# Flamingo block on one core: DVE's selection rounds, the rank matmuls, the roots on GpSimd and SyncE's first loads stand in another order

## The chip, the cores and the metric

The kernel runs on one core of a Trainium2 chip. Its five engines run their own instruction streams: TensorE (PE), VectorE (DVE), ScalarE (ACT), GpSimd (POOL) and SyncE (SP). The metric is device time in microseconds (us) for one execution of the whole program; lower is better.

## The reference

Four gated parts follow each other on `x` of 4 batches x 256 rows x 256 columns: a learned 256 x 256 adjacency per batch, a mixture of 64 experts, a causal attention with 16 heads, and a mixture of 8 experts with a shared one. The change lies in the first two:

```
# adjacency of batch b, h = context, adj_raw = layernorm(x)
threshold = top_k(sim, 76)[..., -1:]
A = sigmoid(sim) * (sim >= threshold)
x = x + tanh(g_xattn[0]) * ((1 - gamma) * layernorm(x) + gamma * (A + A.T) / 2)
# experts, on layernorm(x) as 1024 rows
probs = softmax(xn @ gate_w.T)               # 64 experts
topk_w, topk_idx = top_k(probs, 8)
out = sum over the 8 experts e of  w_e * (silu(xn @ g_e.T) * (xn @ u_e.T)) @ w2_e.T
x = x + tanh(g_ffn[0]) * out
```

## The kernel before

The 1024 rows are `TT` = 8 tiles of 128, two per batch (`BT`). The kernel is written engine by engine, each block in its own order, and the engines meet at named semaphores.

**Routing, per batch b.** PE makes the scores, ACT copies them (`sim_copied`). DVE finds the 76th largest of each row in `ROUNDS` = 10 rounds (`top_rounds`, L1103): a round is a `max` of eight values and a `match_replace` that takes them out, each for two tiles; the last round is a `max` alone. `mask(b)` (L1136) writes `AM`. On PE, `mix(b)` (L526) sums in PSUM the base rows (`ident` times `BASES`), `AM` and `AM` transposed. ACT copies the sum to `X1` (L898, `x1_kept`). `mix_stats(b)` takes mean and variance (`var_ready`), `norm_scale(b)` on POOL takes the root (L432), and `mix_norm(b)` writes the normalised rows `XNA` (L1159). PE's `logits(b)` follows, then DVE's `choose(b)` (L1168), which marks the eight chosen experts of each row in `MB` (bfloat16 zeros and ones, `mask_ready`). PE's `ranks(b)` (L554) counts how many rows ahead of each row chose the same expert: a product of ones with the mask of every earlier tile, and of a strict triangle with its own. `place(b)` (L1180) turns the counts into slot numbers `IDX` (`idx_ready`).

DVE works on the rounds of batch b + 1 in the waits of batch b; the loop at L1199 deals them out by hand. The order of the experts needs the totals `psN` and `psC`, which PE sums at the end over all eight masks (L575 to L579, `counted`).

**Rows to slots.** POOL sends each tile's rows to the slots of their experts in DRAM (`slots_in`), one indirect DMA for each of the eight choices: 16 for a batch, 64 in all (L441 to L449). `norm_scale` of the next batch stands in this stream. A batch's 16 need its `IDX` and `XNA`.

**Experts.** The experts are ordered by load; a place is a position in this order. SP reads the number of the expert at a place (`value_load` of `ORD`, after `order_ready`), loads its weights into `WR` (128 x 768 numbers, L348) and its slots into `XE` (L352). Both are rings of `RING` = 8. The slots wait for all 64 scatters (`scattered`); from the ninth place on, SP waits until the place that held the ring entry is done. For each place PE turns the slots (`flip`, L593), makes gate and up (`gate_up`, L606) and, one place later, down (L616).

Afterwards POOL gathers the results, and attention and the second mixture follow; the change doesn't touch them.

## Time and profile before

| what | value |
|---|---|
| median of 3 runs | 563.95 us (562.79 to 567.25) |
| profiled execution, its own time | 561.23 us |
| its span, first to last instruction | 559.3 us |
| busy: PE, DVE, ACT, POOL | 412.9, 344.4, 184.5, 148.6 us |
| mean granted clock of TensorE | 0.92 |
| first scatter starts, last one starts | 43.22 us, 137.56 us |
| first slots landed, PE starts on them | 142.85 us |

The profile records one execution. Starts are given in us from the span's start; a row of the timeline names engine, line of the kernel, output and inputs, and in brackets how long the engine stood idle before it and what ended that. The profiled execution is 2.7 us shorter than the median of the runs; 1.9 us of its time lie outside its span.

### The profile page before, as it was taken

What the parts mean: (1) busy time and instruction counts of PE and PEld (TensorE: products, weight loads), DVE (VectorE), ACT (ScalarE), POOL (GpSimd) and SP (SyncE); (2) the same over time, 40 slices, a digit from 0 to 9 for tenths busy, and PEclk for the clock granted to TensorE, in tenths of its full rate; (3) what the DMA queues carried; (4) which work ended last, traced back from release to release, by engine and by line L of the source; (5) the groups of instructions that cost most, each with busy time, mean ns of one, the idle gap of its engine ahead of it and who ended that gap; (6) DMA issues with size and microseconds to landing.
All of it is one profiled execution on the core that took longest, in us unless ns stands there. A gap on an engine that the chain in (4) does not pass through costs nothing.

```text
span 559.3 us, 9235 instructions
## 1 busy us (share of the span) xinstructions
PE 412.9 (74%) x2738; PEld 347.8 (62%) x2738; DVE 344.4 (62%) x1053; ACT 184.5 (33%) x377; POOL 148.6 (27%) x156
## 2 busy tenths in 40 slices
PE   5345642500799999999823676799789988998796
PEld 3234441400798888988622554797678867996695
DVE  4988876279334444443346893488667885680664
ACT  3122220100233333343236143524453354427321
POOL 4017775757000000000477723330424000000000
PEclk9999999755699999999965879799999999999999
DMA  7999222237599999999832201110212000000000
GB/s 238 424 416 403 91 94 76 94 112 282 146 293 303 324 317 313 331 355 385 279 98 75 86 22 56 39 39 2 59 39 75 2 0 0 20 1 2 2 19 20
DMA packets 36789, 82.96 MB, mean 148 GB/s; under 512 B 6032, under 2 KB 16144, under 8 KB 34960
## 3 DMA queue, kind: packets, MB, share of 16 engines
q1 hardware_dynamic: 23616, 56.48, 29.2%
q0 software_dynamic: 6144, 16.79, 9.4%
q10 hardware_dynamic: 6992, 9.24, 4.6%
q8 instruction: 17, 0.28, 0.2%
q14 instruction: 20, 0.16, 0.1%
HBM read 50.44 MB, written 31.92 MB: 147 GB/s over the span
## 4 chain that ended last, share of the span: by engine, by line
PE 50%; DVE 13%; issue 12%; POOL 7%; ACT 7%; SPq 4%; DMA 3%; another core or an unknown queue 2%; ACTq 1%; DVEq 0%; POOLq 0%
PE PS L606 9%; POOL slots_in L447 7%; PE PS L616 6%; PE PS L695 5%; PE PS L772 3%; PE PS L708 3%; PE PS L709 3%; PE PS L710 3%; PE PS L593 2%; PE PS L669 2%; DMA XE<-slots_in 2%; PE PS L790 2%; PE PS L800 2%; PE PS L757 2%
## 5 line engine op out<-in xcount | busy, mean ns | idle before, releaser
L454 POOL DMA_INDIRECT GB<-slots_out,IDXG x64 | 70.2, 1096 | 221.1 <-DMA slots_out<-OE 133.3
L606 PE MATMUL PS<-XTE,WR 128*128 128x128 f32 (+2 forms) x512 | 80.5, 301 | 0.0
L447 POOL DMA_INDIRECT slots_in<-XNA,IDX x64 | 64.9, 1014 | 38.3 <-issue 30.8
L606 PEld LDWEIGHTS PS<-XTE,WR 128*128 128x128 f32 x512 | 71.2, 195 | 0.3
L1302 DVE TENSOR_TENSOR HE<-SGE,PS 128x128 f32<-128x128 f32 (+2 forms) x64 | 19.9, 312 | 71.7 <-ACT SGE L927 66.3
L616 PE MATMUL PS<-WR,HE 128*80 128x256 f32 (+2 forms) x198 | 53.3, 380 | 0.5 <-issue 0.5
L918 ACT COPY XTE<-PS 128x256 f32<-128x256 f32 (+2 forms) x64 | 26.3, 410 | 73.1 <-PE PS L593 72.0
L708 PE MATMUL PS<-XH,WGH 128*128 128x256 f32 x160 | 50.3, 314 | 0.0
L593 PE MATMUL PS<-CF,XE 80*128 80x80 f32 (+2 forms) x198 | 28.6, 258 | 26.2 <-DMA XE<-slots_in 26.0
L695 PE MATMUL PS<-WD,XW 128*128 128x256 f32 x160 | 42.6, 389 | 5.8 <-DVE TH L1391 5.8
L593 PEld LDWEIGHTS PS<-CF,XE 80*128 80x128 f32 (+2 forms) x198 | 22.9, 145 | 36.5 <-DMA XE<-slots_in 29.7
L709 PE MATMUL PS<-XL,WGH 128*128 128x256 f32 x160 | 45.5, 284 | 0.0
L710 PE MATMUL PS<-XH,WGL 128*128 128x256 f32 x160 | 45.4, 284 | 0.0
L1295 DVE COPY OE<-PS 128x256 f32<-128x256 f32 (+2 forms) x64 | 36.2, 566 | 8.2 <-PE PS L616 5.5
L979 ACT ACTIVATE AM<-PS 128x256 f32<-128x256 f32 x40 | 15.3, 383 | 68.9 <-PE PS L710 68.8
L1391 DVE SCALAR_TENSOR_TENSOR TH<-PS,CM,TH 128x256 f32<-128x256 f32 x72 | 31.5, 479 | 4.4 <-PE PS L695 3.9
L695 PEld LDWEIGHTS PS<-WD,XW 128*128 128x128 f32 x160 | 27.9, 193 | 9.2 <-DVE XW L1398 4.3
L927 ACT ACTIVATE SGE<-PS 128x128 f32<-128x128 f32 (+2 forms) x64 | 18.9, 296 | 43.9 <-PE PS L606 43.9
L616 PEld LDWEIGHTS PS<-WR,HE 128*80 128x80 f32 (+2 forms) x198 | 30.0, 165 | 5.2 <-issue 0.9
L1473 DVE TENSOR_REDUCE NM<-PS 128x2 f32<-128x256 f32 x64 | 31.6, 549 | 2.4 <-PE PS L775 2.2
L1347 DVE SCALAR_TENSOR_TENSOR BASE<-GB,W,BASE 128x256 f32<-128x256 f32 x56 | 26.7, 485 | 10.1 <-DMA GB<-slots_out,IDXG 5.5
L708 PEld LDWEIGHTS PS<-XH,WGH 128*128 128x128 f32 x160 | 30.9, 193 | 1.1 <-issue 0.6
(226 smaller groups left out, 814.9 us busy)
## 6 DMA issues: line engine op xcount, KB each, us to landing
WR<-in_wexp SPq DMA_DIRECT2D x64, 384.0 KB
slots_in<-GB SPq DMA_DIRECT2D x12, 1024.0 KB, 18.5
XE<-slots_in SPq DMA_DIRECT2D x24, 160.0 KB, 4.4
slots_out<-OE ACTq DMA_DIRECT2D x24, 160.0 KB
XE<-slots_in SPq DMA_DIRECT2D x29, 128.0 KB, 4.3
slots_out<-OE ACTq DMA_DIRECT2D x24, 128.0 KB
WGU<-in_wgu SPq DMA_DIRECT2D x1, 2560.0 KB
XE<-slots_in SPq DMA_DIRECT2D x11, 192.0 KB, 4.1
```

The costliest lines, as they stand in the source:

```text
L447: pool.indirect_dma_start(out=xs, out_offset=bass.IndirectOffsetOnAxis(ap=IDX[:, t, j:j + 1], axis=0), in_=XNA[:, t, :], in_offset=None, b ...
L454: pool.indirect_dma_start(out=GB[:, t % BT, j, :], out_offset=None, in_=ys[0:rows, :], in_offset=bass.IndirectOffsetOnAxis(ap=IDXG[:, t, j ...
L593: last = nc.tensor.transpose(psXE[place % 2][:, k, r * rows:(r + 1) * rows], XE[0:rows, place % RING, r, k * P:(k + 1) * P], ident[0:rows, ...
L606: last = mm(psGE[place % 2][:, a, 0:cap(place)], W13[:, k, a, :], XTE[:, place % 2, k, 0:cap(place)], start=(k == 0), stop=(k == KC - 1))
L616: last = mm(psOE[place % 2][0:rows, r, :], HE[:, place % 2, r * rows:(r + 1) * rows], WR[:, place % RING, 2 * D:3 * D], start=True, stop=True)
L695: last = mm(psW[:, t, :], H1[:, c % 2, t * P:(t + 1) * P], WD1[:, c, :], start=True, stop=True)
L708: mm(dst, WGH[:, c, k, a, :], XH[:, k, :], start=(k == 0), stop=False)
L709: mm(dst, WGH[:, c, k, a, :], XL[:, k, :], start=False, stop=False)
L710: last = mm(dst, WGL[:, c, k, a, :], XH[:, k, :], start=False, stop=(k == KC - 1))
L1295: V.tensor_copy(OE[0:rows, place % ORING, 0:parts, :], psOE[place % 2][0:rows, 0:parts, :]).then_inc(S["oe_copied"], 1)
L1391: last = V.scalar_tensor_tensor(FA[:, t, :], psW[:, t, :], w, so_far[:, t, :], ALU.mult, ALU.add)
L1473: last = V.tensor_reduce(NM[:, t, u * 2:(u + 1) * 2], ps1[:, u % 2, :, t * P:t * P + (t + 1) * P], AX.X, ALU.max, negate=True)
```

## The change

It edits five things in the routing and at its end.

1. **Rounds.** For batches 1 and 2 of the loop, `top_rounds` of the next batch is split as 3, 2, 3, 1, 1 rounds (ahead of the statistics, the normalisation, the choice, the placing, and behind it) where it was 2, 1, 2, 1, 4. In batch 0's turn it stays 1, 2, 2, 1, 4.
2. **Base rows.** `mix(b)` runs the base product of both tiles ahead of its wait for `masked`, where the second one stood in the middle.
3. **Ranks.** DVE keeps `MSUM`, the running sum of the masks of all earlier tiles, and PE multiplies ones with this sum once, where it went through every earlier mask. In the last batch, `psN` and `psC` are made from it, ahead of the ranks, and `counted` is gone.
4. **Roots.** The root of batches 2 and 3 stands behind 7 scatters of the batch ahead, where it stood behind 10. Batch 1's stays behind 10.
5. **SP.** It reads the numbers and loads the weights of three places (`AHEAD`) ahead of the rows. Numbers, slots and weights of the other five places of the ring follow behind the first three loads of slots.

```diff
-POW_AT = 2
+ROOT_BEHIND = (None, 10, 7, 7)
+AHEAD = 3
+FIRST_ROUNDS = (1, 3, 5, 6)
+LATER_ROUNDS = (3, 5, 8, 9)
...
-            first = [expert(e) for e in range(RING)]
-            for e in range(RING):
+            first = []
+            for e in range(AHEAD):
+                first.append(expert(e))
                 load_weights(e, first[e])
             sp.wait_ge(S["scattered"], 16 * TT * TOP0)
-            for e in range(RING):
+            for e in range(AHEAD):
                 load_slots(e, first[e])
+            for e in range(AHEAD, RING):
+                n = expert(e)
+                load_slots(e, n)
+                load_weights(e, n)
...
-                    if t % BT == BT - 1 and j == POW_AT and t // BT + 1 < B:
-                        norm_scale(t // BT + 1)
+                    b = t // BT + 1
+                    if b < B and t % BT * TOP0 + j == ROOT_BEHIND[b]:
+                        norm_scale(b)
...
                 for t in range(BT):
-                    mm(psT[:, t, :], ident, BASES[b % 2][:, t, :], start=True, stop=False)
-                    if t == 0:
-                        pe.wait_ge(S["masked"], b + 1)
+                    mm(psT[:, t, :], ident, BASES[b % 2][:, t, :], start=(t == 0), stop=False)
+                pe.wait_ge(S["masked"], b + 1)
+                for t in range(BT):
                     mm(psT[:, t, :], ident, AM[:, t, :], start=False, stop=False)
...
             def ranks(b):
+                pe.wait_ge(S["idx_ready"], b)
+                if b:
+                    pe.wait_ge(S["masks_added"], b)
                 pe.wait_ge(S["mask_ready"], b + 1)
-                pe.wait_ge(S["idx_ready"], b)
+                own = [MB[:, b * BT + t, :] for t in range(BT)]
+                if b == B - 1:
+                    parts = [MSUM[:, :]] + own
+                    for i, part in enumerate(parts):
+                        mm(psN, onesb, part, start=(i == 0), stop=(i == BT))
+                    for i, part in enumerate(parts):
+                        mm(psC, part, onesb[:, 0:1], start=(i == 0), stop=(i == BT))
                 for t in range(BT):
-                    n = b * BT + t
-                    for m in range(n):
-                        mm(psR[:, t, :], onesb, MB[:, m, :], start=(m == 0), stop=False)
-                    last = mm(psR[:, t, :], before, MB[:, n, :], start=(n == 0), stop=True)
+                    earlier = ([MSUM[:, :]] if b else []) + own[0:t]
+                    for i, part in enumerate(earlier):
+                        mm(psR[:, t, :], onesb, part, start=(i == 0), stop=False)
+                    last = mm(psR[:, t, :], before, own[t], start=(not earlier), stop=True)
                 last.then_inc(S["ranked"], 1)
...
+                if b == 0:
+                    V.tensor_tensor(MSUM[:, :], MB[:, 0, :], MB[:, 1, :], ALU.add).then_inc(S["masks_added"], 1)
+                elif b < B - 1:
+                    dve.wait_ge(S["masks_added"], b)
+                    st.done(V.tensor_tensor(MSUM[:, :], MSUM[:, :], MB[:, b * BT, :], ALU.add))
+                    st.wait()
+                    V.tensor_tensor(MSUM[:, :], MSUM[:, :], MB[:, b * BT + 1, :], ALU.add).then_inc(S["masks_added"], 1)
```

The adds to `MSUM` stand at the end of `place`; the wait for `counted` ahead of the experts' order becomes one for the last `ranked`.

On DVE, between the slot numbers of batch 1 and the mask of batch 2 (`TOP` and `WORK` belong to the rounds of batch 2), there stood:

```order
L1192 TENSOR_SCALAR IDX<-K8 128x16
L1110 MAX TOP<-WORK 128x8 x2
L1114 MATCH_REPLACE WORK<-TOP,WORK 128x256 x2
L1110 MAX TOP<-WORK 128x8 x2
L1114 MATCH_REPLACE WORK<-TOP,WORK 128x256 x2
L1110 MAX TOP<-WORK 128x8 x2
L1114 MATCH_REPLACE WORK<-TOP,WORK 128x256 x2
L1110 MAX TOP<-WORK 128x8 x2
L1142 SCALAR_TENSOR_TENSOR AM<-SIM,TOP,TH 128x256 x2
```

and there stands now:

```order
L1210 TENSOR_SCALAR IDX<-K8 128x16
L1216 TENSOR_TENSOR MSUM<-MSUM,MB 128x64
L1218 TENSOR_TENSOR MSUM<-MSUM,MB 128x64
L1128 MAX TOP<-WORK 128x8 x2
L1160 SCALAR_TENSOR_TENSOR AM<-SIM,TOP,TH 128x256 x2
```

Three full rounds have gone from here to places ahead of batch 1's slot numbers, and two adds have come.

On POOL, the 64 scatters and the roots of batches 1, 2 and 3 in a row; there stood:

```order
L447 DMA slots_in<-XNA,IDX 12288x256 x10
L434 TENSOR_SCALAR RS<-MV 128x2
L436 TENSOR_TENSOR RS<-RS,MINUS_HALF 128x2
L447 DMA slots_in<-XNA,IDX 12288x256 x16
L434 TENSOR_SCALAR RS<-MV 128x2
L436 TENSOR_TENSOR RS<-RS,MINUS_HALF 128x2
L447 DMA slots_in<-XNA,IDX 12288x256 x16
L434 TENSOR_SCALAR RS<-MV 128x2
L436 TENSOR_TENSOR RS<-RS,MINUS_HALF 128x2
L447 DMA slots_in<-XNA,IDX 12288x256 x22
```

and there stands now:

```order
L460 DMA slots_in<-XNA,IDX 12288x256 x10
L446 TENSOR_SCALAR RS<-MV 128x2
L448 TENSOR_TENSOR RS<-RS,MINUS_HALF 128x2
L460 DMA slots_in<-XNA,IDX 12288x256 x13
L446 TENSOR_SCALAR RS<-MV 128x2
L448 TENSOR_TENSOR RS<-RS,MINUS_HALF 128x2
L460 DMA slots_in<-XNA,IDX 12288x256 x16
L446 TENSOR_SCALAR RS<-MV 128x2
L448 TENSOR_TENSOR RS<-RS,MINUS_HALF 128x2
L460 DMA slots_in<-XNA,IDX 12288x256 x25
```

Counted within its batch, the second root has moved from behind 10 scatters to behind 7, and so has the third.

On PE, from the last batch's logits to the experts' order, there stood:

```order
L551 MATMUL PS<-GATE0,XNT 128x64 x4
L560 MATMUL PS<-MB,CB 128x64 x6
L561 MATMUL PS<-MB,CB 128x64
L560 MATMUL PS<-MB,CB 128x64 x7
L561 MATMUL PS<-MB,CB 128x64
L576 MATMUL PS<-MB,CB 128x64 x8
L578 MATMUL PS<-CB,MB 64x1 x8
L581 MATMUL PS<-OH,CB 128x64
L582 MATMUL PS<-DG,CB 128x64
```

and there stands now:

```order
L564 MATMUL PS<-GATE0,XNT 128x64 x4
L577 MATMUL PS<-MSUM,CB 128x64
L577 MATMUL PS<-MB,CB 128x64 x2
L579 MATMUL PS<-CB,MSUM 64x1
L579 MATMUL PS<-CB,MB 64x1 x2
L583 MATMUL PS<-MSUM,CB 128x64
L584 MATMUL PS<-MB,CB 128x64
L583 MATMUL PS<-MSUM,CB 128x64
L583 MATMUL PS<-MB,CB 128x64
L584 MATMUL PS<-MB,CB 128x64
L599 MATMUL PS<-OH,CB 128x64
L600 MATMUL PS<-DG,CB 128x64
```

The last ranks take 5 matmuls where they took 15, and the six for the totals have moved from behind them (where they were 16) to ahead of them.

## Rows read from the trace of the kernel before

**Rows 1.** The page of the profile: the chain that ended last.

```profile
PE 50%; DVE 13%; issue 12%; POOL 7%; ACT 7%; SPq 4%; DMA 3%; another core or an unknown queue 2%; ACTq 1%; DVEq 0%; POOLq 0%
```

**Rows 2.** The chain in order of time: start us, length us, what.

```profile
12.27 0.65 DVE TOP L1110 x2
...
12.93 0.79 DVE WORK L1114 x2
...
26.70 0.85 PE PS L530 x2
...
137.56 2.42 DMA slots_in<-XNA,IDX
...
140.15 2.66 DMA XE<-slots_in
```

**Rows 3.** Timeline, GpSimd (POOL): start, length, line, what, idle before.

```profile
66.47 0.97 POOL L447 DMA_INDIRECT slots_in<-XNA,IDX  x1 [1.75 <-issue]
...
91.44 0.97 POOL L447 DMA_INDIRECT slots_in<-XNA,IDX  x1 [3.77 <-DVE IDX L1192]
...
116.30 0.97 POOL L447 DMA_INDIRECT slots_in<-XNA,IDX  x1 [3.67 <-DVE IDX L1192]
...
120.13 1.46 POOL L447 DMA_INDIRECT slots_in<-XNA,IDX  x1 [0.30 <-issue]
```

**Rows 4.** Timeline, batch 2 from its mask to its slot numbers.

```profile
65.44 0.17 DVE L1192 TENSOR_SCALAR IDX<-K 128x16 int32<-128x16 f32 x1
...
68.81 0.60 ACT L877 ACTIVATE GB<-PS 128x512 f32<-128x512 f32 x1 [2.16 <-PE PS L523]
...
70.72 0.88 DVE L1142 SCALAR_TENSOR_TENSOR AM<-SIM,TOP,TH 128x256 f32<-128x256 f32 x2
...
76.33 0.58 ACT L898 COPY X<-PS 128x512 f32<-128x512 f32 x1 [4.42 <-PE PS L535]
...
77.73 0.25 DVE L1154 BATCH_NORM_AGGREGATE MV<-ST 128x2 f32<-128x6 f32 x2
...
80.13 0.74 DVE L1163 TENSOR_SCALAR XNA<-X,MV,RS 128x256 f32<-128x256 f32 x2 [0.73 <-POOL RS L436]
...
80.22 1.07 POOL L447 DMA_INDIRECT slots_in<-XNA,IDX  x1 [0.19 <-issue]
...
84.72 0.36 DVE L1172 MAX8 L<-PS 128x8 f32<-128x64 f32 x2 [0.97 <-PE PS L551]
...
85.72 0.29 DVE L1178 TENSOR_TENSOR MB<-PS,LR 128x128 bf16<-128x128 f32 x1
...
89.38 0.29 DVE L1185 TENSOR_TENSOR KEY<-PS,CF 128x128 f32<-128x128 f32 x1 [1.93 <-remote]
```

**Rows 5.** Timeline, slot numbers of batches 1 and 3.

```profile
64.41 0.28 DVE L1185 TENSOR_TENSOR KEY<-PS,CF 128x128 f32<-128x128 f32 x1
...
109.69 0.36 DVE L1172 MAX8 L<-PS 128x8 f32<-128x64 f32 x2 [3.86 <-PE PS L551]
...
114.23 0.29 DVE L1185 TENSOR_TENSOR KEY<-PS,CF 128x128 f32<-128x128 f32 x1 [3.25 <-remote]
```

**Rows 6.** Timeline, loads by SyncE (SP) and the fourth place's matmuls.

```profile
122.61 4.28 SPq L348 DMA_DIRECT2D WR<-in_wexp  x8
...
153.61 1.49 PE L606 MATMUL PS<-XTE,WR 128*128 128x192 f32 x8
```

**Rows 7.** Busy time in stretches; after the engines: granted clock, DMA share, GB/s.

```profile
140.00:145.00 5.00, 2.15 (x10) 1.90 (x11) 2.37 (x4) 0.96 (x2) 0.00 (x0) 0.50 0.73 206
145.00:150.00 5.00, 5.00 (x21) 4.91 (x20) 0.35 (x1) 0.81 (x2) 0.00 (x0) 0.55 0.45 112
150.00:155.00 5.00, 5.00 (x34) 4.53 (x33) 2.08 (x4) 1.62 (x4) 0.00 (x0) 1.00 0.56 162
...
240.00:260.00 20.00, 19.84 (x149) 17.31 (x148) 7.93 (x25) 7.79 (x24) 0.00 (x0) 1.00 1.03 372
...
290.00:306.00 16.00, 4.76 (x12) 3.24 (x12) 9.53 (x24) 10.92 (x5) 11.62 (x10) 0.50 0.28 77
```

More of the change, by code:

```diff
@@ L268, in gated_block @@
             gu_done silu_done h_done o_done o_used
[L269 removed]
+            zero_set zeroed mask_ready masks_added ranked idx_ready scattered order_set order_done order_ready flag_ready w8_ready
             all_stored general_done gb_used xt_flipped xt_copied gue_done silue_done he_done oe_done oe_copied dve_w8
@@ L529, in mix @@
                 for t in range(BT):
-                    mm(psT[:, t, :], ident, BASES[b % 2][:, t, :], start=True, stop=False)
-                    if t == 0:
-                        pe.wait_ge(S["masked"], b + 1)
+                    mm(psT[:, t, :], ident, BASES[b % 2][:, t, :], start=(t == 0), stop=False)
+                pe.wait_ge(S["masked"], b + 1)
+                for t in range(BT):
                     mm(psT[:, t, :], ident, AM[:, t, :], start=False, stop=False)
                     for c in range(BT):
-                        last = mm(psT[:, t, c * P:(c + 1) * P], AM[:, c, t * P:(t + 1) * P], ident, start=False, stop=(c == BT - 1))
+                        last = mm(psT[:, t, c * P:(c + 1) * P], AM[:, c, t * P:(t + 1) * P], ident, start=False, stop=(t == BT - 1 and c == BT - 1))
                 last.then_inc(S["summed"], 1)
@@ L573, in _ @@
                     scores(b + 2)
-            for n in range(TT):
-                last = mm(psN, onesb, MB[:, n, :], start=(n == 0), stop=(n == TT - 1))
-            for n in range(TT):
-                last = mm(psC, MB[:, n, :], onesb[:, 0:1], start=(n == 0), stop=(n == TT - 1))
-            last.then_inc(S["counted"], 1)
             pe.wait_ge(S["order_set"], 1)
@@ L1213, in _ @@
                 if ahead:
-                    top_rounds(b + 1, 3, 5)
+                    top_rounds(b + 1, to_norm, to_choose)
                 choose(b)
                 if ahead:
-                    top_rounds(b + 1, 5, 6)
+                    top_rounds(b + 1, to_choose, to_place)
                 place(b)
                 if ahead:
-                    top_rounds(b + 1, 6, ROUNDS)
+                    top_rounds(b + 1, to_place, ROUNDS)
             st.end()
             st = Steps(dve, S["dve_w8"])
-            dve.wait_ge(S["counted"], 1)
+            dve.wait_ge(S["ranked"], B)
             experts = slice(0, E0)
```

7 lines of the change are left out of this document (4 added, 3 removed).

## The prediction

> **What bounds the kernel now.** I read the chain that ended last first. Over the whole span half of it is PE [rows 1], but the change lies ahead of the experts, so the question is what carries the chain there. In order of time it is DVE's rounds, then the scatters on GpSimd, then the last scatter at 137.56, its landing, the first load of slots at 140.15 and PE at 140.15 + 2.66 = 142.8 [rows 2]. From there on PE runs through the experts, so whatever makes the last scatter earlier makes everything behind it earlier, one for one.
>
> The timeline of GpSimd tells why the last scatter is that late. A scatter takes 0.97 and the next follows 0.30 later [rows 3], which makes 1.28 with rounding. A batch's 16 and one root (also 1.28, below) are 17 x 1.28 = 21.8. Yet the first scatters of batches 1, 2 and 3 start at 66.47, 91.44 and 116.30 [rows 3]: distances of 25.0 and 24.9, so some 3.1 of each are waiting. Both waits (3.77 and 3.67) end with DVE's `IDX`. So GpSimd is nearly full, and the slot numbers of batches 2 and 3 come 3 us too late for it. The most that better order can give here is those two waits, 6.3 us. Batch 3's own stretch, 116.30 to 137.56, is 21.3 and stays.
>
> **Prices.** A full round is 0.65 + 0.79 = 1.44 for two tiles [rows 2]. From the end of `IDX` (65.44 + 0.17) to the mask at 70.72 [rows 4] are 5.1: three full rounds and a last maximum of 0.8. One tile's base product is 0.85 on the path [rows 2]. From mask to ACT's copy of the sum are 76.33 - 71.60 = 4.73; with the second base product out, 3.88. From that copy to `var_ready` are 77.98 - 76.33 = 1.65. A root that is ready to run takes from 78.94 (80.22 less 1.28) to the next scatter at 80.22, and `XNA` starts 0.1 ahead of that, so 1.19 behind the last scatter [rows 4]. From `XNA` to the choice are 4.59, from the choice to the end of `MB` 1.29, and from `KEY` to the first scatter 91.44 - 89.38 = 2.06 [rows 3, 4].
>
> **Batches 0 and 1.** The rounds are dealt as before in batch 0's turn; one base product less is 0.85 at most ahead of its slots. I take nothing of it into the sum, for batch 1's choice now has three rounds ahead of it: `XNA` 0.65, then 4.33, so 4.98 behind the start of `XNA` where it was 4.59. That loses 0.4 of what the base products bring. Batch 1's first scatter stays at 66.5, give or take 0.4.
>
> **Batch 2.** Behind `IDX` at 65.6 there are two adds, at most 0.3 each (a `KEY` of twice the size takes 0.28 [rows 5]), and a last maximum: the mask is done by 68.0, where it was 71.6. But PE can't use all of that. It makes the scores of batch 3 until 68.8 (ACT copies them then [rows 4]) and now two base products, 1.7, to 70.5. The sum is copied at 70.5 + 3.88 = 74.4, two us earlier, and `var_ready` is at 76.0. GpSimd has put out seven scatters by 66.5 + 7 x 1.28 = 75.4, and stands 0.6 at the root with nine scatters queued behind it; it goes on at 77.3 and is free for the next batch's scatters at 77.3 + 9 x 1.28 = 88.8. DVE has two rounds, 2.9, between statistics and `XNA`, so `XNA` starts at 78.9 (80.13 before); three rounds more, and the choice is at 83.9 (84.72 before), DVE being last and no longer PE. `MB` is done at 85.2.
>
> Now the one stretch that I can't price. In batch 2, `KEY` starts 89.38 - 86.01 = 3.37 after `MB` is done, and DVE stood idle 1.93 of that; in batch 3 it is 114.23 - 110.98 = 3.25, all idle [rows 4, 5]. The ranks are 11 and 15 matmuls there. In batch 1 they are 7, and `KEY` starts at 64.41 with no idle time ahead of it [rows 5]. The new ranks are 5. Upper end: 3.37 stays, for 11 matmuls and 15 cost the same, and what batches 2 and 3 share is that no scores follow on PE. Lower end: it vanishes, as in batch 1, and `KEY` comes behind the round at 86.7. I take the upper end, since four more matmuls added nothing. (The Trainium skill, Perfetto Trace Analysis, section on the Tensor Engine Instruction, says that a matmul's end in a profile is estimated from its size and that the semaphore comes when PSUM has acknowledged; the idle rows agree that PE's part ended later than its rows say. If that time went with the matmuls, 5 for 11 would bring the lower end, a gain of 5.7.)
>
> Upper: `KEY` 88.6, first scatter of batch 2 at 90.6. Lower: `KEY` 86.7, scatter 88.8 (GpSimd free 88.8). Before: 91.44.
>
> **Batch 3.** With the upper end: `IDX` done 89.8, adds and last maximum 1.4, mask 0.9, so 92.0; copy of the sum 95.9; `var_ready` 97.6. Seven scatters are out at 90.6 + 8.96 = 99.6, so the root doesn't wait. `XNA` 100.8, choice 105.4, `MB` 106.7, `KEY` 109.9 with 3.25 kept, first possible scatter 112.0. GpSimd itself is free at 90.6 + 21.8 = 112.4. So it no longer waits at all, and the root's three places forward are what buys this: behind ten scatters `XNA` would be 3.8 later and the scatter would wait till 115.8. With the lower end GpSimd is free at 110.6, and `IDX` allows 110.1. First scatter of batch 3: 112.4 or 110.6 for 116.30. **Gain 3.9, or 5.7.**
>
> **Totals ahead of the ranks.** 6 and 5 matmuls before `ranked` for 15: nothing, as GpSimd is the last one there. The experts' order comes 4 earlier and is needed only behind the scatters.
>
> **Adds and GpSimd.** The scatter at 120.13, beside DVE's wide two-input operations, takes 1.46 for 0.97 [rows 3], so DVE can hold it up. The adds fall where GpSimd waits for the first scatter, so 0; if all five met one, 5 x 0.3 = 1.5 at most. Batch 3's stretch has the same DVE work beside it as before. (SBUF — State Buffer in the Trainium skill, section Who interferes with whom, has this rule: a DVE instruction with two inputs in SBUF and a GpSimd one that reads SBUF exclude each other. The row agrees; by the rule the sum would be 2.4 to 3.9 in the upper case.)
>
> **SP.** Eight numbers and eight loads of weights become three ahead of the rows; a load takes 4.28 / 8 = 0.54 to issue [rows 6]. Behind the rows SP issues three loads of slots, then five times number, slots, weights: at most 0.7 + 0.54 + 0.54 = 1.8 each (0.7: eight numbers between order and 122.61). The fourth place's weights are issued by 140.15 + 1.6 + 1.8 = 143.6 and the eighth's by 150.8 on the old clock; the fourth place's gate and up start at 153.61 and take 1.49 [rows 6], so the eighth's can't start ahead of 159.6. DMA has room: 27%, 55% and 44% of it are free between 140 and 155 [rows 7], 6.3 us in all, and five weights of 0.39 MB are 2.0 MB, at 372 GB/s [rows 7] 5.3 us. PE isn't kept waiting. Cost 0. The scatters gain nothing from quieter queues, for their rows are bound by issue.
>
> **Sum.** 0 - 3.9 + 0 = -3.9 on the profiled execution: 561.23 - 3.9 = 557.3. The median shown is 2.7 above that execution, and against it I give 563.95 - 3.9 = **560.0**.
>
> **Rivals.**
> - *The ranks' lag goes with the matmuls.* Gain 5.7, 558.3. For it: batch 1 with 7 matmuls shows no lag. Against: 11 and 15 cost alike.
> - *The moved loads meet a full DMA stage* (the other side). The share is 1.03 between 240 and 260 [rows 7], and 2.0 MB that were moved unseen at 122 to 137 now come behind 140. If they don't fit the free 6.3 us, DMA runs up to 5.3 us late through the experts, and once the ring's lead is eaten PE waits: 560.0 + 5.3 = 565.3, slower than before by 0.2%. It decides from the point at which the fourth to eighth weights come more slowly than PE goes from place to place. For it: 5.3 of 6.3 is tight. Against: PE is still busy for 19.84 of those 20 us [rows 7], so a lead was left.
> - *TensorE's clock.* It is granted at half at PE's start on the slots (0.50, 0.55) and again at 290 to 306 [rows 7], and an earlier start may meet another pattern. PE's first 7 us on the experts, from 142.8 on, lie almost wholly at the half level; at the full one they would be up to 3.5 shorter, and as much again at half costs as much. Some 3 us either way, on top of the forecast: 557 to 563; with long half stretches in attention 10 us, 570.
> - *Nothing moves*: GpSimd stands at the earlier root, which decides from `var_ready` later than 75.4 on, each us one for one. Over 4 us late (the old time was 77.98) it would eat the gain: 564.
>
> **Chances.** Forecast 0.45, the lag gone 0.28, the clock taking or giving over 2 us 0.14, loads late 0.07, nothing 0.06. A difference of 1%, 5.6 us, is about what a measurement can tell. Only the lag's end with a little more passes it: faster 0.28; slower by 1% needs the long half stretches: 0.04; the rest 0.68. The range takes in both ends of the lag, two us of clock to either side, and the late loads all but their worst: 556.0 to 564.5.
>
> **What would show it.** Right: batch 3's first scatter at 112.4 (or 110.6), no wait ahead of it; the root of batch 2 with 0.6 idle ahead; choice of batch 2 at 83.9; `KEY` 3.3 behind `MB` with 5 matmuls; PE's first slots 3.9 earlier and no wait at L606's counterpart for weights. Wrong: scatters that still wait for `IDX`, PE idle in the fourth to eighth place, or a larger half-clock share.

## The result: 1.0% slower where it was measured first, and 0.3 to 0.7% faster on other chips

The changed kernel takes 569.66 us (median of 20 runs, 565.1 to 638.09), the kernel before 564.12 us (20 runs, 561.93 to 568.78) beside it. The ratio is 1.0096, 95% interval 1.0075 to 1.0116: slower by 5.5 us, where 3.9 us less were forecast and 564.5 was the top of the range. The profiled execution takes 568.98 us, its span is 567.2. (All ratios leave out executions that are over 1.5% above the fastest of the same kernel, as the one of 638.09 here; five of u3's twelve and three of u4's eight go out by that, their two traces, at 566.6 and 571.3 us, among them.)

What the prediction summed up did happen. The timeline of the changed kernel (start, length, engine, line, what, idle before): the last root, SyncE's loads of weights, one of DVE's operations, the last scatter, and PE on the first places:

```profile
101.31 0.22 POOL L446 TENSOR_SCALAR RS<-MV 128x2 f32<-128x2 f32 x1 [4.52 <-DVE MV L1172]
...
114.54 14.11 SPq L355 DMA_DIRECT2D WR<-in_wexp  x3
...
114.70 0.68 DVE L1287 TENSOR_TENSOR KEY<-KEY,ROW 128x512 f32<-128x512 f32 x1
...
133.32 1.12 POOL L460 DMA_INDIRECT slots_in<-XNA,IDX  x1 [0.30 <-issue]
...
138.68 1.54 PE L611 MATMUL PS<-CF,XE 96*128 96x96 f32 x8 [26.23 <-DMA XE<-slots_in]
...
152.25 2.02 PE L634 MATMUL PS<-WR,HE 128*96 128x256 f32 x4 [7.01 <-DVE HE L1329]
...
158.68 1.49 PE L624 MATMUL PS<-XTE,WR 128*128 128x192 f32 x8
```

The last scatter starts at 133.32 where it was 137.56 [rows 2], 4.2 earlier, although GpSimd waits 4.52 at the third root, which the forecast put at nothing. PE's start on the slots has moved with it, from 142.85 (the end of the load in [rows 2]) to 138.68. Then PE loses all of that and more. It stands 7.01 us ahead of the first down product (L634) and waits for `HE`, DVE's product for the first place. The fourth place's gate and up start at 158.68; they started at 153.61 [rows 6]. So 4.2 ahead have become 5.1 behind. The chain that ended last, in order of time (start, length, what), says why `HE` is late:

```profile
84.49 14.99 another core or an unknown queue
99.50 0.59 ACT X L916
...
115.38 1.33 issue
116.71 0.72 DVE KEY L1289
...
118.85 0.23 DVE K L1292
119.08 7.49 another core or an unknown queue
126.57 1.42 issue
127.99 0.25 DVE IDXG L1294
...
134.29 0.70 DVE EQ L1308
...
151.02 0.75 DVE W L1313
151.80 0.04 issue
151.84 0.36 DVE HE L1329
```

In the kernel before, DVE had time to spare there:

```profile
141.79 0.69 DVE L1286 TENSOR_REDUCE W<-EQ 128x8 f32<-128x512 f32 x1
...
147.64 0.35 DVE L1302 TENSOR_TENSOR HE<-SGE,PS 128x192 f32<-128x192 f32 x1 [5.17 <-ACT SGE L927]
```

In DVE's order the weights of the experts (`EQ`, `W`, three operations for each of eight tiles, 17.5 us) stand ahead of the first `HE`. In r1 below, another run of the changed kernel, 5.5 us lie between the start of L1287 (110.00) and that of the first `EQ` (115.52). Here L1287 starts at 114.70, so by that pace the weights should begin at 120.2; they begin at 134.29. DVE is busy for 4.5 of the 18 us from 115 to 133, in r1 for 17.0. The 7.49 is put down to "another core or an unknown queue", on a program of one core: no releaser that the trace knows. The eight maxima `K` that `IDXG` needs had ended at 119.08. The same at ACT: the sum of batch 3 is complete at 96.2 (the end of PE's L548) and is copied at 99.50. And at SyncE, whose three loads of weights take 14.11 us to issue where eight took 4.28 [rows 6].

I call such a time a **stretch**: DVE, ACT and SyncE wait long for semaphores though the work that they wait for is over by the trace, while GpSimd issues scatters every 1.28 us. In the changed kernel there are two, from 86 to 99.5 and from 114.5 to 134.3. With that seen, the 1.93 and 3.25 us of idle DVE ahead of `KEY` in the kernel before [rows 4, 5], which I could not price, look like short ones.

### The profile page after: what moved, and what is told of

Its sections match the earlier page's. It is cut to its first block, busy times and chain, and to the rows that moved or that the text cites. A ratio compares the mean times of both kernels' runs of the same rounds, so it can differ in the third digit from the quotient of the medians.

```text
span 567.2 us, 9184 instructions
## 1 busy us (share of the span) xinstructions
PE 414.1 (73%) x2710; PEld 350.6 (62%) x2710; DVE 344.2 (61%) x1058; ACT 184.5 (33%) x377; POOL 145.9 (26%) x156
## 4 chain that ended last, share of the span: by engine, by line
PE 49%; DVE 20%; issue 11%; ACT 7%; SPq 5%; another core or an unknown queue 4%; DMA 2%; DVEq 0%; POOL 0%; ACTq 0%; POOLq 0%
PE PS L624 7%; PE PS L634 6%; PE PS L713 5%; DVE WORK L1132 3%; DVE TOP L1128 3%; PE PS L726 3%; PE PS L728 3%; PE PS L727 3%; PE PS L790 3%; PE PS L687 2%; PE PS L611 2%; PE PS L808 2%; PE PS L775 2%; SPq L352 2%
## 5 line engine op out<-in xcount | busy, mean ns | idle before, releaser
L467 POOL DMA_INDIRECT GB<-slots_out,IDXG x64 | 68.8, 1076 | 234.0 <-DMA slots_out<-OE 141.7
L460 POOL DMA_INDIRECT slots_in<-XNA,IDX x64 | 63.2, 988 | 32.4 <-issue 18.6
L634 PE MATMUL PS<-WR,HE 128*80 128x256 f32 (+2 forms) x198 | 54.5, 387 | 7.3 <-DVE HE L1329 7.3
L634 PEld LDWEIGHTS PS<-WR,HE 128*80 128x80 f32 (+2 forms) x198 | 30.5, 169 | 12.5 <-DVE HE L1329 8.0
```

Of the source, the lines that this page charges most:

```text
L460: pool.indirect_dma_start(out=xs, out_offset=bass.IndirectOffsetOnAxis(ap=IDX[:, t, j:j + 1], axis=0), in_=XNA[:, t, :], in_offset=None, b ...
L467: pool.indirect_dma_start(out=GB[:, t % BT, j, :], out_offset=None, in_=ys[0:rows, :], in_offset=bass.IndirectOffsetOnAxis(ap=IDXG[:, t, j ...
L634: last = mm(psOE[place % 2][0:rows, r, :], HE[:, place % 2, r * rows:(r + 1) * rows], WR[:, place % RING, 2 * D:3 * D], start=True, stop=True)
```

## The experiments

Eighteen runs, in six groups; each group ran on one chip, beside runs of the kernel before, no two groups on the same one. What is called the chip's below can so be the time's as well. "Gather indices" is the start of DVE's `IDXG`, "first product" that of the first `HE`, "experts" the end of the last `HE`; all in us in the profiled execution. In the first two rows stand the two traces already shown.

| run | before beside it | ratio, interval | last scatter | gather indices | first product | experts |
|---|---|---|---|---|---|---|
| before | 564.12 | | 137.56 | 121.92 | 147.64 | 275.53 |
| changed | 564.12 | 1.0096, 1.0075 to 1.0116 | 133.32 | 127.99 | 151.84 | 279.56 |
| p1 | 558.47 | 1.0098, 1.0057 to 1.0139 | 139.20 | 119.21 | 149.37 | 275.75 |
| d1 | 558.47 | 1.0036, 0.9994 to 1.0078 | 135.91 | 115.21 | 145.83 | 272.87 |
| d2 | 558.47 | 1.0120, 1.0066 to 1.0173 | 137.63 | 115.09 | 147.49 | 274.48 |
| u1 | 558.47 | 0.9948, 0.9914 to 0.9982 | 133.54 | 115.01 | 143.49 | 269.61 |
| r0 (before) | 559.75 | 0.9990, 0.9951 to 1.0028 | 133.31 | 117.67 | 143.80 | 270.63 |
| r1 (changed) | 559.75 | 0.9950, 0.9912 to 0.9989 | 131.12 | 112.58 | 140.92 | 266.47 |
| b1 | 559.75 | 0.9977, 0.9941 to 1.0013 | 134.30 | 118.67 | 144.31 | 271.06 |
| u2 | 559.75 | 1.0016, 0.9974 to 1.0058 | 134.24 | 118.60 | 144.29 | 272.01 |
| r2 (changed) | 561.98 | 0.9969, 0.9938 to 0.9999 | 132.35 | 123.59 | 146.77 | 271.54 |
| u3 | 561.98 | 0.9994, 0.9953 to 1.0035 | 133.42 | 124.67 | 150.13 | 277.57 |
| u4 | 561.98 | 0.9915, 0.9876 to 0.9953 | 131.34 | 135.81 | 156.22 | 283.30 |
| r3 (changed) | 558.32 | 0.9953, 0.9919 to 0.9988 | 131.30 | 112.77 | 141.13 | 266.81 |
| w1 | 558.32 | 0.9940, 0.9896 to 0.9985 | 130.27 | 113.10 | 140.25 | 266.61 |
| d1b | 558.32 | 1.0042, 1.0003 to 1.0080 | 136.00 | 115.29 | 146.09 | 272.31 |
| u1b | 558.32 | 0.9961, 0.9922 to 0.9999 | 133.20 | 114.67 | 143.37 | 269.68 |
| w1b | 561.13 | 0.9919, 0.9892 to 0.9947 | 134.01 | 120.81 | 143.94 | 270.87 |
| r4 (changed) | 558.70 | 0.9933, 0.9899 to 0.9968 | 131.31 | 112.78 | 141.24 | 267.17 |
| w1c | 558.70 | 0.9980, 0.9950 to 1.0010 | 130.09 | 112.93 | 140.40 | 267.49 |

### First group: is it the queue ahead of GpSimd?

p1 holds GpSimd back to three scatters in flight:

```diff
+                    turn, sent = divmod(t * TOP0 + j, 3)
+                    if turn:
+                        pool.wait_ge(S["sent%d" % sent], 16 * turn)
                     pool.indirect_dma_start(...)
-                        .then_inc(S["scattered"], 16)
+                        .then_inc(S["sent%d" % sent], 16)
...
```

> The changed kernel, with GpSimd held back: a scatter is not issued before the third one ahead of it has landed, so GpSimd's stream never runs more than three scatters ahead. Nothing is left out. In the changed kernel DVE, ACT and SyncE show waits of 0.6 to 2 us between instructions from about the 32nd scatter to the pause at 97 us, and from the 48th (114.5 us) until the last scatter ends (134.4 us); DVE's weights for the experts end at 151.7 us, and TensorE waits for them. Theory Depth (the queue of scatters ahead of GpSimd causes these waits): they are gone, the weights end at about 143 us, the fourth place's matmuls start at about 150 us in place of 158.7, and the time is 560 to 563 us. Rival Count (something happens at every sixteenth scatter, whatever the depth): the waits stay, and the time with them, 568 to 571 us. Rival Moved loads or clock: the waits of DVE go but the time stays above 567 us.

d1 and d2 make it pause until all has landed, at three places:

```diff
+                    if t * TOP0 + j in (16, 32, 48):     # d2: (24, 40, 56)
+                        pool.wait_ge(S["scattered"], 16 * (t * TOP0 + j))
```

> The changed kernel, but GpSimd waits ahead of the 17th, 33rd and 49th scatter until all scatters before have landed. Nothing is left out. A scatter takes 1.28 us from start to start and lands 2.42 us after its start, so each such wait costs some 1.2 to 2 us and the last scatter starts 4 to 6 us later than the 133.3 us of the changed kernel, as late as in the kernel before. Theories Depth and Count both say that the long stretches of slow engines shrink to what the kernel before shows (about 2 us at a batch's last scatter): weights of the experts end at 143 to 146 us and the time is 562 to 565 us. If the slow engines come from the moved SyncE loads or the ranks instead, nothing changes but the scatters: 569 us or more.

> As the kernel with waits at the 17th, 33rd and 49th scatter, but with the same three waits ahead of the 25th, 41st and 57th one. Nothing is left out. Theory Count in its absolute form (it begins at the 32nd and the 48th scatter and lasts until GpSimd pauses): slow engines from about 86 us to 97 us and from about 115 us for some 10 us more, in place of 20; the time is between the two, 564 to 568 us. Theory Depth, or a count that starts again at each pause: no long slow stretch, or one that begins 16 scatters behind a pause (after the 40th and 56th, that is at the pauses themselves): 562 to 565 us.

u1 takes the new deal of rounds back: `LATER_ROUNDS = (2, 3, 5, 6)`.

> The changed kernel with the old deal of the rounds (2, 1, 2, 1, 4 in batches 1 and 2); all else as changed. Nothing is left out. The slot numbers of batches 2 and 3 then come 2 to 4 us later, so GpSimd runs dry between the batches as in the kernel before. Theories Depth and Count: the slow stretches shrink, and the time falls to 563 to 566 us though a part of the change that was to bring a gain is taken out. Rivals (moved loads, ranks, clock): the time stays at 569 us or rises by the 3 to 4 us that the scatters lose.

All four traces were without stretches, and u1's ratio, 0.9948, was below one. But u1's GpSimd had no pause at all from the 24th scatter to the 64th except for a root, with the next batch's scatters queued behind the running ones. So neither the depth of the queue nor the count of scatters is enough to make a stretch, and both theories fall in the form in which I had put them. The times expected for the four were meant for the chip of the result; that p1's 562.81 falls within its 560 to 563 says nothing. Whether pauses would shorten a stretch was not learned: there was none to shorten. What the pauses cost could be read: d1's last scatter starts 4.8 us later than r1's, and its ratio is 0.009 above the changed kernel's; d2's starts 6.5 later, at 0.017 above. (These compare chips; d1b below, beside the changed kernel on one chip, gives 0.009 and 4.4 us too, within the 2 to 5 forecast for it.) In p1 the fourth scatter starts 5.4 us behind the third, because it waits for landings while the DMA engines are full: four scatters between 42 and 52 us take 7.9 us to land in the median, against 2.4 over the whole run. The zeroing of the slots is over by then, as GpSimd had waited for it until 42.86; SyncE's loads of later weights, issued by 32.8, are not (`WGU` lands 22.9 us behind its issue at 29.71).

### Second group: does it belong to the program?

> The changed kernel once more, unedited, beside the others of this group. With the old deal of the rounds it had run at 0.995 of the kernel before, with no slow stretch, though its scatters followed each other as closely as in the changed kernel: what is queued ahead of GpSimd can't be the whole cause. Theory Program: the slow stretches belong to the program with its new deal of rounds; they stand here again from about the 32nd scatter to GpSimd's pause and from the 48th to the last one's end, and the ratio is 1.007 to 1.012. Rival Chip or execution: they come and go from one execution or chip to the next; this trace shows none, and the ratio falls to 0.99 to 1.00.

> The kernel before once more, unedited, for its trace beside the others. Both theories: ratio 1.000. Theory Program: its trace shows the same 3.3 us from mask to slot numbers' start at batches 2 and 3 that it showed before, where batches 0 and 1 take 1.36 us. Rival Chip or execution: the 3.3 us are gone here.

The changed kernel, unedited, ran at 0.995. The timeline of this trace, beside the chain shown above:

```profile
109.03 2.60 SPq L355 DMA_DIRECT2D WR<-in_wexp  x3
109.50 0.97 POOL L460 DMA_INDIRECT slots_in<-XNA,IDX  x1 [0.30 <-issue]
...
110.00 0.68 DVE L1287 TENSOR_TENSOR KEY<-KEY,ROW 128x512 f32<-128x512 f32 x1
110.71 0.69 DVE L1289 TENSOR_TENSOR KEY<-KEY,MB 128x512 f32<-128x512 f32 x1
110.78 1.47 POOL L460 DMA_INDIRECT slots_in<-XNA,IDX  x1 [0.30 <-issue]
111.44 1.11 DVE L1292 MAX8 K<-KEY 128x8 f32<-128x64 f32 x8
112.58 0.26 DVE L1294 TENSOR_SCALAR IDXG<-K,FM 128x64 int32<-128x64 f32 x1
...
132.17 0.69 DVE L1313 TENSOR_REDUCE W<-EQ 128x8 f32<-128x512 f32 x1
...
140.92 0.35 DVE L1329 TENSOR_TENSOR HE<-SGE,PS 128x192 f32<-128x192 f32 x1 [8.06 <-ACT SGE L945]
```

From the maxima to the gather indices are 0.03 us of idle time where there were 8.91, and the weights end 8 us ahead of the first product. SyncE issues the three loads of weights in 2.60 us.

The kernel before on this chip has lost its lag too; the timeline of DVE in r0, which answers to [rows 4] and [rows 5]:

```profile
87.21 0.28 DVE L1185 TENSOR_TENSOR KEY<-PS,CF 128x128 f32<-128x128 f32 x1
...
109.98 0.29 DVE L1185 TENSOR_TENSOR KEY<-PS,CF 128x128 f32<-128x128 f32 x1 [1.14 <-PE PS L561]
```

`MB` ends at 85.86 and 108.83, so 1.35 and 1.15 us for 3.37 and 3.25, with the old ranks of 11 and 15 matmuls. The lag was no price of the matmuls alone; on this chip some 2 us of it are gone (u4 below says more). Theory Program falls; the rival, chip or execution, stands.

b1 has the new rounds alone, in the kernel before; u2 is the changed kernel with `ROOT_BEHIND = (None, 10, 10, 10)`:

```diff
-                    top_rounds(b + 1, 0, 2 if b else 1)
+                    top_rounds(b + 1, 0, 3 if b else 1)
...
-                    top_rounds(b + 1, 3, 5)
+                    top_rounds(b + 1, 5 if b else 3, 8 if b else 5)
```

> The kernel before with the new deal of the rounds alone (3, 2, 3, 1, 1 in batches 1 and 2). Nothing is left out. The rounds are DVE's work ahead of the slot numbers of batches 1 and 2: three more stand ahead of them, three fewer behind. Theory Program with the deal of rounds as the cause: slower than before by 0.5 to 1.5 per cent (567 to 572 us where before takes 564), with slow stretches in its trace. By the prediction's sum, which knew no slow stretches, the deal brings the mask of batches 2 and 3 some 2 to 4 us forward and the time would fall by 0.3 to 0.7 per cent. Rival Together (slow stretches need the new ranks or roots too): no slow stretch here, ratio 0.993 to 1.000.

> The changed kernel with the root of batches 2 and 3 behind 10 scatters again. Nothing is left out. The statistics of batch 2 are ready at 74.7 us and the 10th scatter of batch 1 ends some 4 us later, so normalised rows and slot numbers of batches 2 and 3 come 3 to 4 us later, behind the end of the queued scatters. Theory that close-packed scatters together with early slot numbers make the slow stretches: they shrink and the ratio is 0.995 to 1.003. Rival Rounds alone: slow stretches as in the changed kernel, ratio 1.007 or more.

Neither differs clearly from the kernel before; b1's 0.9977 leaves the 0.3 to 0.7% that the prediction's sum gave it open, but its last scatter didn't come forward. Both last scatters (134.30, 134.24) are 0.9 later than r0's 133.31: with the root behind ten scatters, more rounds ahead of the slot numbers only push these back. The new roots without the new rounds (u1, on another chip) end at 133.54. Only together do they bring 131.12. But the last scatter isn't the whole of the gain: u1's starts no earlier than r0's, and its ratio is 0.9948 all the same.

### Third group: a chip with stretches

> The changed kernel unedited, a third time. Its first trace had slow stretches (DVE's idle time of 8.9 us ahead of the gather indices at 119 to 128 us) and a ratio of 1.010; its second, on another chip, had none and a ratio of 0.995. The kernel before shows the like in small: 3.3 us from mask to slot numbers in its first trace, 1.36 and 1.15 us in its second. Theory Chip: the slow stretches belong to the chip; where the kernel before takes some 564 us on the chip of this group, they are here and the ratio is 1.007 to 1.012; where it takes some 559 us, they are not and the ratio is 0.991 to 0.999. Rival Execution: trace and ratio don't go with the time of the kernel before.

> The changed kernel with SyncE's old loads: numbers and weights of all eight places ahead of the rows. Nothing is left out. SyncE then issues eight loads of weights between about 108 and 125 us beside the scatters, and the eight loads of slots follow each other at 0.5 to 0.7 us from 133 us on. Prediction's view (the new order of SyncE costs nothing): the same time as the changed kernel beside it, within 1 us. Rival: the moved loads are what brings or costs; 2 to 5 us away from it, and the fourth place's matmuls start that much earlier or later.

> The changed kernel with the old ranks: no running sum, products with every earlier mask, the totals at the end. Nothing is left out. Prediction's view: the ranks of batches 2 and 3 take some 0.3 to 0.6 us more on TensorE, the experts' order comes later by the 16 small products (about 1 us) and is covered by the scatters, which end at the same time; so within 1 us of the changed kernel beside it. Rival Lag (the 2 us more between mask and slot numbers at batches 2 and 3 go with the number of the ranks' matmuls): slot numbers of batches 2 and 3 start 3.3 us behind the masks and the time rises by 2 to 4 us.

u3 sets `AHEAD = 8`; u4 has the old `ranks(b)`, the totals at the end with `counted`, and no `MSUM`. All three traces have stretches. Theory Chip had no branch for what r2 shows, a kernel before at 562 us, stretches, and a ratio of 0.997. In r2 the gather indices wait 7.34 us and the first product again waits for the weights (their end 146.69, `HE` at 146.77, PE on the slots since 137.88).

u3 shows where SyncE's old order can cost. The first line is the timeline, the others are pieces of the chain in the same trace, about 0.7 us each:

```profile
113.37 27.09 SPq L355 DMA_DIRECT2D WR<-in_wexp  x8
```

```profile
129.51 0.70 SPq L355
130.22 0.69 issue
130.91 0.70 SPq L355
...
140.66 4.63 DMA XE<-slots_in
145.33 1.61 PE PS L611 x8
```

SyncE is still busy with numbers and weights when the last scatter's row ends (134.63), so the first slots are asked for at 140.66, 7.2 us behind the last scatter's start; in r2 (`AHEAD` = 3) it is 2.9 (135.29), in r1 2.8. The experts end 6.0 us later than in r2. But this is the trace of one of the executions that the ratio leaves out; the ratios of u3 and r2 are 0.0025 apart, 1.4 us, with intervals that overlap. A cost of the old order on this chip is seen in one trace and not shown in the times.

u4 has the deepest stretch. The timeline at batch 2's slot numbers, and the chain between batch 3's slot numbers and the experts' order, which needs `counted`:

```profile
88.45 0.29 DVE L1198 TENSOR_TENSOR KEY<-PS,CF 128x128 f32<-128x128 f32 x1 [3.17 <-remote]
```

```profile
110.12 0.07 DVE IDX L1205
110.19 12.21 another core or an unknown queue
122.40 0.02 issue
122.42 0.22 DVE CKR L1240
```

Yet of its eight timed executions only three are like this one (570.3 to 572.4 us); five take 555.9 to 560.5, and the ratio, 0.9915, the lowest of the group, is of these five alone. So on this chip the same program can go either way, and one trace says little on an edit. Of the rival Lag: `KEY` of batches 2 and 3 comes 4.6 and 2.8 behind `MB` here, and 1.2 to 1.4 in the four traces that have stretches and the new ranks (the changed kernel's first, r2, u3, w1b). With the old ranks r0, without stretches, has 1.35 and 1.15. So the lag stands where old ranks and stretches meet, in both traces that have both (this one and the kernel before), and nowhere else. The new ranks may so take away a wait that only stretches bring; two traces don't prove it.

### Fourth to sixth group: the weights behind the first places

```diff
-            for t in range(TT):
+            def weights(t):
                 ...
-            st.end()
+            weights(0)
+            weights(1)
...
                 if place:
                     copy_out(turn, place - 1)
+                if place in (1, 3, 5, 7, 9, 11):
+                    weights(2 + place // 2)
+                if place == 12:
+                    st.end()
```

> The changed kernel unedited, as the measure for the others of this group. So far two chips showed slow stretches in its trace (ratio 1.010 and 0.997, kernel before at 564 and 562 us) and one showed none (ratio 0.995, kernel before at 559.8 us). Theory Chip: a chip on which the kernel before takes some 559 us shows none and gives 0.991 to 0.999; one on which it takes 562 us or more shows them, and gives 0.996 to 1.012.

> The changed kernel with DVE's last six of the eight tiles of experts' weights (13 us of its work) moved from ahead of the first place's product to behind places 1, 3, 5, 7, 9 and 11. Nothing is left out. Where slow stretches hold DVE back, the weights end at 147 to 152 us in the changed kernel and the first place's product waits for them, though its slots are there at 138.7 us. Theory Chain (the slow stretches cost time through this chain alone): the first product starts at 142 to 144 us, and the kernel is 3 to 8 us faster than the changed kernel beside it. Without slow stretches the weights end at 132.9 us, 8 us ahead of the first product: then no difference within 1 us. Rival: the experts' start is held by something else that the stretches slow, and nothing is gained; or the weights in between hold up the places' products and cost 1 to 3 us.

> The changed kernel with GpSimd's wait for all landed scatters ahead of the 17th, 33rd and 49th, again, beside the changed kernel on the same chip. On a chip without slow stretches it costs the 4.8 us by which the last scatter starts later, 2 to 5 us in all. On a chip with them, theory Pause (a pause of GpSimd lets the other engines catch up): the stretches end at each pause, DVE's gather indices start at 115 to 118 us in place of 124 to 128, and it is as fast as the changed kernel or up to 5 us faster. Rival: the stretches don't care for pauses, it is slower there too by 2 to 5 us.

> The changed kernel with the old deal of the rounds, again, beside the changed kernel on the same chip. On another chip it ran at 0.995 of the kernel before, as the whole change did on a third. If the new deal brings nothing, the two are within 1 us here, on any chip. By the trace without slow stretches the new deal brings the last scatter 2.4 us forward (131.1 against 133.5 us), so it should be slower by 2 to 3 us. On a chip with slow stretches the rival Deal (the new rounds deepen the stretches): 3 to 8 us faster than the changed kernel.

> The changed kernel with six of DVE's eight tiles of experts' weights behind places 1 to 11, once more, in the hope of a chip that shows slow stretches. Nothing is left out. There, theory Chain: DVE's gather indices start at 123 us or later as in the changed kernel, yet the first place's product starts within 6 us of TensorE's start on the slots (in the changed kernel 13.2 us behind it), and the ratio to the kernel before is 0.985 to 0.995, as on chips without the stretches (0.994), where the changed kernel gave 0.997 and 1.010. Rival: the product is late all the same, and the ratio is 0.997 or more. On a chip without slow stretches: 0.990 to 0.998 again, which tells nothing new.

> The changed kernel unedited, beside the one with DVE's weights behind the first places. On a chip without slow stretches 0.991 to 0.999 of the kernel before, its gather indices at 113 us; on a chip with them 0.996 to 1.012, its gather indices at 120 us or later.

> The changed kernel with six of DVE's eight tiles of experts' weights behind places 1 to 11. Nothing is left out. On a chip with slow stretches, theory Chain: 2 to 8 us faster than the changed kernel beside it, its first product within 6 us of TensorE's start on the slots. Rival: within 1 us of it. On a chip without them: within 1 us of it by both.

The fourth and the sixth group fell on chips without stretches. The changed kernel gives 0.9953 and 0.9933, within the 0.991 to 0.999 that Theory Chip gave such a chip; w1 gives 0.9940 and 0.9980: no difference that both groups show (w1c is 2.3 us above r4 in the median, where 1 us was allowed for, with intervals that overlap). d1b is 4.4 us above r3. u1b is 1.2 us above r3 in the median, where its last scatter, 1.9 us later, let one expect 2 to 3; the intervals overlap, so it is not shown that the new deal of rounds gains anything in time. The fifth group, w1b alone, fell on a chip with stretches and gave 0.9919 (0.9892 to 0.9947), below the changed kernel's 0.9969 and 1.0096 on two such chips (the interval of the first, 0.9938 to 0.9999, just overlaps). Its timeline, DVE and PE:

```profile
120.81 0.25 DVE L1294 TENSOR_SCALAR IDXG<-K,FM 128x64 int32<-128x64 f32 x1 [3.19 <-remote]
...
139.15 1.57 PE L611 MATMUL PS<-CF,XE 96*128 96x96 f32 x8 [26.85 <-DMA XE<-slots_in]
...
143.94 0.35 DVE L1331 TENSOR_TENSOR HE<-SGE,PS 128x192 f32<-128x192 f32 x1 [14.76 <-ACT SGE L945]
...
146.13 1.03 PE L634 MATMUL PS<-WR,HE 128*96 128x256 f32 x4
```

`HE` waits for ACT and no longer for the weights. But in this execution the stretch at the gather indices was short, and by 124.87, the start of the first tile, plus 8 x 2.17 all eight tiles would have ended at 142.2, ahead of 143.94. So of what theory Chain expected, the ratio and the first product within 6 us of PE's start came (4.8), the gather indices at 123 or later did not, and the trace alone doesn't decide, and the edit never ran beside the changed kernel on a chip with stretches. It beats the kernel before there; that it beats the changed one is likely by the ratios and not shown.

## Why the prediction was wrong, step by step

**The step that failed** is one sentence that was sized at nothing: "The experts' order comes 4 earlier and is needed only behind the scatters". It costed DVE's work from batch 3's slot numbers to the weights as covered by the scatters. In the kernel before it is: its weights end at 142.5, 5.2 us ahead of the first product at 147.64. That margin is the cover, and I never wrote it down, nor what it costs if it is gone. On the chip of the result the second stretch puts the weights back by 14.1 us (134.29 for 120.2) and eats it; they end at 151.7, 13 us behind PE's start on the slots, PE stands 7.01 us, and the end of the experts moves from 275.53 to 279.56 in place of 271.6. With the cover falls the rule that whatever makes the last scatter earlier makes all behind it earlier, one for one: 4.2 us earlier there became 4.0 later at the end of the experts. Behind it stands an assumption that no part of the sum names: that DVE, ACT, PE and SyncE keep their pace while GpSimd scatters.

**The unpriced lag.** I took the upper end (3.37 us stay) since 15 matmuls cost no more than 11. The lower came in: `KEY` starts 1.35 and 1.31 behind `MB`. The rival had the size right, and for the cause it is at best half right: by r0 it is not the matmuls alone, by u4 the old ranks may have a part in it where there are stretches. What r0 keeps at batch 3 is a wait of 1.14 us for PE; the other 2.1 of the 3.25 were not PE's. Idle time that the trace puts down to "remote" in a program of one core should have been a sign that its cause lay outside this stretch of code, and so could move.

**Batch 1 and 2.** First scatters at 66.60 (66.5 forecast) and 88.16 (90.6, or 88.8 by the lower end). The sum is copied at 73.09 (74.4), the root doesn't wait (0.6), the choice is at 82.49 (83.9): 1.3 to 1.4 earlier than forecast.

**Batch 3.** The copy is at 99.50 (95.9), and the root waits 4.52 (0), by the first stretch. The rival "nothing moves" named this wait at the root, but it took only a part of the gain: the first scatter of batch 3 starts at 114.13 for 116.30 (112.4 or 110.6 forecast). The last one still comes 4.2 earlier: beside a DVE that stands still, sixteen scatters take 19.2 us from first to last start, 21.3 in the kernel before and 21.6 in r1. So half of the 4.2 lies in batch 3's own scatters, which the forecast left as they were; that its 3.9 is so near is luck.

**SP at cost 0.** Not contradicted: no run without stretches has the old order beside the rest of the change, and with stretches one trace has the first slots asked for 4.3 us later behind the last scatter with the old order (u3 against r2). PE waits for no weights in places four to eight, so the rival of the full DMA stage did not come.

**TensorE's clock.** The mean granted clock fell from 0.92 to 0.856, but that is hardly a cause here: r0, the kernel before on another chip, has 0.861 at a span of 554.5 us. The fall lies ahead of 135 us (0.65 for 0.89), mostly under the scatters, where PE has little to do; from there to the end of the experts it is 0.93 for 0.95. Behind the experts the clock does cost; see below.

**The gain itself** is real where there are no stretches. There the signs of being right come in: in r1 the first scatters of batches 2 and 3 start at 88.00 and 109.50 with no wait ahead of them (88.8 and 110.6 by the lower end). From r0 to r1, r3 and r4 the last scatter moves by 2.0 to 2.2 us (not 3.9: the kernel before has no lag to lose there, and its GpSimd waits 1.74 and 1.53 for `IDX` where it was 3.77 and 3.67), and the experts end 3.5 to 4.2 us earlier; of the other 1.5 to 2 us, r1 against r0 shows 1.6 in PE's first three places: r0 waits 0.43 for a second load of slots, and its gate and up, turn, gate and up take 2.82, 0.85 and 1.92 for 2.48, 0.50 and 1.49, at a granted clock of 0.50 for 1.00 between 140 and 144. The ratios are 0.9950, 0.9953 and 0.9933, 2.6 to 3.7 us, a little under the forecast's 3.9. In the two profiled executions of the result the spans differ by 7.9 us (5.5 between the medians): 4.0 of it up to the end of the experts. The other 3.9, behind it, is within what two executions of one kernel differ by (below).

**Range and chances.** The 0.04 for slower by 1% came from long half-clock stretches alone. No rival had an engine's waits growing as GpSimd's gaps closed, though the profile had 5 us of idle DVE without a named cause in the very place that the change squeezes.

**What stays open** is the cause of the stretches. They go by the chip, or by the time at which its group ran: on three chips all six traces have them (the two first ones taken as of one chip, and that chip as none of the others), on four chips none of fourteen. On those three the fastest runs of the kernel before are at 558.2 to 561.9 us, on the four at 553.2 to 554.5. All that I found lie within GpSimd's scatters. Two marks go with them in the traces. One: the landings of the scatters are missing, in all six and in none of the fourteen. More is lost: the six hold 4,449 to 4,579 records of landings, the fourteen 5,805 to 5,808, and those of the engines' own semaphore updates are fewer too (6,315 in the changed kernel's first trace, 7,821 in r1), from 40 us on, also where no engine is late. So an unnamed releaser in the six can be a lost record; the idle time ahead of it is real. The list of DMA issues (line, engine, count, median us from issue to landing), first of the changed kernel's own trace, then of r1:

```profile
slots_in<-XNA,IDX POOLq DMA_INDIRECT x64
```

```profile
slots_in<-XNA,IDX POOLq DMA_INDIRECT x64, 2.4
```

Two: SyncE's steps in u3 are about 0.70 us apart, and go on so until 137.2, 2.6 us behind the end of the last scatter's row. Whether the semaphore updates (16 a scatter in the code) have a part in it, or the recording of the trace, nothing here tests. Nor was it tested whether a pause of GpSimd ends a stretch. The four traces with a long first stretch (the changed kernel's first, r2, u3, w1b) hint at it: GpSimd ends its seventh scatter of batch 2 at 96.7 to 97.0 and then stands, and ACT's late copy comes 1.0 to 2.7 us behind that. But the gather indices of the second stretch come while the scatters go on.

## What to carry to other kernels

Work that is "covered" has a margin in us; write it into the sum, and ask what a slower engine does to it, above all if a change closes the gaps of the engine that covers it. Idle time without a named releaser is not a constant of the code: before an edit is built on it, look whether a second trace from another chip has it. And a change of 1% or less to a kernel with such waits wants more than one chip: this one is at 1.010, 0.997 and 0.993 to 0.995 on five.

## What the runs showed of the hardware

The span behind the experts differs by 5.8 us between two executions of the same changed kernel, on two chips: 550.1 - 266.81 = 283.3 in r3 and 556.3 - 267.17 = 289.1 in r4. Two pieces of that time (window, length, busy time of PE, PEld, DVE, ACT, POOL; granted clock, DMA share, GB/s), first r3, then r4:

```profile
300.00:330.00 30.00, 22.98 (x161) 17.53 (x159) 25.07 (x61) 10.57 (x21) 13.16 (x13) 0.77 0.19 55
330.00:360.00 30.00, 23.48 (x145) 19.77 (x145) 13.99 (x49) 13.28 (x22) 10.37 (x10) 0.89 0.16 45
```

```profile
300.00:330.00 30.00, 23.99 (x140) 18.94 (x140) 23.95 (x51) 9.30 (x17) 14.28 (x14) 0.65 0.18 53
330.00:360.00 30.00, 23.62 (x118) 18.24 (x119) 10.14 (x42) 11.34 (x21) 8.37 (x9) 0.66 0.12 35
```

With the granted clock at 0.65 and 0.66 for 0.77 and 0.89, PE gets through 258 matmuls where r3 gets through 306. This is larger than the whole effect of the change.

In r1 (above) the scatter at 110.78, beside DVE's wide operations with two inputs, takes 1.47 us, the one ahead of it 0.97. That the same 16 scatters are 2.4 us shorter in the changed kernel's first trace, where DVE stands still, is the other side of it. (SBUF — State Buffer in the Trainium skill, section Who interferes with whom, has DVE instructions with two inputs in SBUF and GpSimd ones that read SBUF exclude each other; the trace agrees: 1.47 us for 0.97.)
